# An eight-batch attention stack on one core: loads split and reordered, stacks loaded in quarters, a rewritten end, and new item orders

## The reference, cut to what matters

```python
sa = mha(x, x, swq, sbq, ..., mask=(j <= i) & (i - j < 64), bias=slopes * (j - i))
x  = layernorm(x + sa, g1, be1)
ca = mha(x, ctx, cwq, cbq, ...)                  # 512 keys, no mask
x  = layernorm(x + ca, g2, be2)
x  = layernorm(x + gelu(x @ w1 + b1) @ w2 + b2, g3, be3)
# second layer: 512 keys, a key mask
q, c = rmsnorm(x) * g_q, rmsnorm(ctx) * g_c
out  = rmsnorm(x + mha(q, c, Wq, Wk, Wv, Wo, key_mask), g_out)
```

## Time and profile before

| | |
|---|---|
| median of 3 runs | 595.97 us (595.77 to 596.03) |
| the profiled execution's own time | 598.34 us |
| span of its trace | 596.5 us |
| TensorE busy | 535.9 us, 90% of the span |
| VectorE busy | 440.7 us, 74% |
| ScalarE busy | 424.8 us, 71% |
| GpSimd busy | 340.3 us, 57% |
| mean granted TensorE clock | 0.958 of full |

### The profile page before, as it was taken

One profiled execution on the slowest core, in us unless ns is written; L12 is line 12 of the kernel. 1 busy time (PEld: TensorE's weight loads), 2 busy tenths in 40 slices (PEclk: granted clock), 3 DMA queues, 4 the chain that ended last, 5 costly groups with the idle time before them and its releaser, 6 DMA issues.

```text
span 596.5 us, 17406 instructions
## 1 busy us (share of the span) xinstructions
PE 535.9 (90%) x6868; PEld 293.6 (49%) x6868; DVE 440.7 (74%) x884; ACT 424.8 (71%) x658; POOL 340.3 (57%) x642
## 2 busy tenths in 40 slices
PE   3377989887899999999999999999999999998983
PEld 1255666663444444555554545454555444443431
DVE  6234656554989998888878788888787898989911
ACT  2135555553087887789889898989898888786782
POOL 5434578883372744646477767585858556362051
PEclk9669999996689999999999999999999999999998
DMA  6664445554515527242433435261707081643000
GB/s 175 165 162 111 112 111 150 149 159 85 134 61 123 150 31 178 92 90 96 84 116 66 129 52 144 38 157 24 174 10 178 11 184 43 137 127 47 11 12 18
DMA packets 85335, 61.08 MB, mean 102 GB/s; under 512 B 5682, under 2 KB 84834, under 8 KB 85218
## 3 DMA queue, kind: packets, MB, share of 16 engines
q1 hardware_dynamic: 85096, 59.87, 41.6%
q10 hardware_dynamic: 158, 0.10, 0.1%
HBM read 33.13 MB, written 26.22 MB: 100 GB/s over the span
## 4 chain that ended last, share of the span: by engine, by line
PE 71%; DVE 7%; DMA 6%; POOL 4%; issue 4%; ACT 2%; SPq 2%; ACTq 1%; POOLq 0%; DVEq 0%
PE pv L585 20%; PE dps L566 14%; PE aps L526 10%; PE dps L656 4%; DVE negmax L840 4%; DMA kst<-k_parts 3%; PE dps L673 3%; PE aps L638 3%; DMA qst<-mT 3%; PE aps L617 3%; DVE negmax L836 3%; PE aps L626 2%; PE dps L661 2%; PE dps L548 2%; PE aps L614 1%
## 5 line engine op out<-in xcount | busy, mean ns | idle before, releaser
L840 DVE TENSOR_REDUCE negmax<-dps 128x1 f32<-128x512 f32 x512 | 322.0, 683 | 45.0 <-PE dps L566 42.8
L708 ACT ACTIVATE probs<-aps 128x1024 f32<-128x1024 f32 x288 | 283.9, 1025 | 56.5 <-PE aps L526 31.7
L585 PE MATMUL pv<-probs,vp 128*32 128x256 f32 (+1 forms) x3072 | 160.1, 335 | 0.4 <-ACT probs L708 0.4
L566 PE MATMUL dps<-kst,qst 61*128 61x512 bf16 x512 | 123.4, 395 | 8.4 <-DMA kst<-k_parts 2.8
L526 PE MATMUL aps<-qst,kst 64*128 64x256 bf16 x1024 | 97.2, 273 | 2.3 <-ACT probs L708 1.1
L585 PEld LDWEIGHTS pv<-probs,vp 128*32 128x32 f32 x3072 | 70.9, 111 | 56.7 <-issue 27.8
L930 POOL TENSOR_SCALAR mcap<-negmax 128x16 f32<-128x16 f32 x48 | 12.1, 253 | 149.8 <-DVE negmax L840 61.7
L566 PEld LDWEIGHTS dps<-kst,qst 61*128 61x128 bf16 x512 | 32.5, 94 | 80.3 <-DVE negmax L840 62.1
L526 PEld LDWEIGHTS aps<-qst,kst 64*128 64x128 bf16 x1024 | 39.1, 94 | 48.8 <-ACT probs L708 18.7
L836 DVE TENSOR_REDUCE negmax<-dps 128x4 f32<-128x512 f32 x64 | 41.2, 686 | 23.0 <-PE dps L557 22.8
L956 POOL TENSOR_TENSOR qr<-qf,qs 128x256 f32<-128x256 f32 x24 | 16.1, 671 | 48.4 <-ACT qs L728 30.1
(11 more groups left out here) (126 smaller groups left out, 769.5 us busy)
## 6 DMA issues: line engine op xcount, KB each, us to landing
kst<-k_parts SPq DMA_DIRECT2D x32, 384.0 KB, 6.2
qst<-q_parts SPq DMA_DIRECT2D x48, 192.0 KB, 3.8
k_parts<-ks SPq DMA_DIRECT2D x16, 384.0 KB, 2.7
...
```

The lines of the kernel that those rows point to most:

```text
L566: mm = nc.tensor.matmul(dve_entry("X", u.index, n + g), q[rows_in(g, 0, ROW_M), four, tile * P:(tile + 1) * P], k[rows_in(g, 0, ROW_M), fo ...
L585: mm = nc.tensor.matmul(pv[32 * j:32 * j + 32, dst:dst + n], vp[u.parity][:, c, 4 * quad + j, :], probs[:, quad, src:src + n], start=(quad ...
L708: nc.scalar.activation(probs[:, quad, part * 1024:(part + 1) * 1024], src, ACT.Exp, scale=SCALE).then_inc(act_emptied, 1)
L840: ins = nc.vector.tensor_reduce(negmax[:, tile, at:at + 1], src, AX.X, ALU.max, negate=True)
```

## The change

Eight new order strings (only `FIRST_STEP` and `LAST_STEP` stay). The start is cut up: only the first batch's x, the identity, the first three weight matrices, two small columns and the second batch's x are issued at once by SP; `identb` and `band` go on ScalarE's queue. Stack 0's constant rows are shared between ScalarE (ones: 4 DMAs) and SP (slopes and mask: 6), stacks 1 and 2 are copied from stack 0 inside SBUF (`copy_rows`, 4 DMAs each). The other weights, the copies, the constants and x of batches 2 to 7 are issued at the head of step -1, the feed-forward weights at step 0. `load_stacks` loads `kst` with four DMAs instead of two; the first two count for `stacks_loaded`, the others for `stacks_rest`, which the ninth pair of maxima of a cross unit (the third of a self unit) waits for. `early` no longer holds for step -1. The last unit's normalisation goes to VectorE, but for the power, and its result is stored by two DMAs, one from SP and one from ScalarE.

```diff
-SECOND_STEP = "XC Q B K X X V M0 X X"
-SELF = "XC B3 Q raw K M1 S D S X P0 X V A P1 S M0 X S P2 X O"
-LAST_SELF = "XC S M1 K V B3 S X raw X Q X X X S P0 X P1 X P2 X S X X M0 X X D X X A X O X"
-CROSS_FFN = ("S X XC X S B3 S X Q X S raw sq0 M1 K X H X D X P0a A X P0b X S S F S X S P1a S X S P1b S X M0 S O "
-             "sq1 V X S sq2 P2a X T S P2b X S S X P3a")
-CROSS = ("XC S X B3 S X raw Q X K X S P0a X S M1 S D S X P0b S X S P1a X S S X P1b X sq0 V X A M0 S O S X S "
-         "P2a S X P2b X sq1 S S X T sq2 P3a X")
-NEXT_SELF = "XC B3 Q raw K M1 S D S X P0 X V A P1 S M0 X S P2 X O"
-FIRST_CROSS = ("XC S X B3 S X raw Q X K X S P0a X S M1 S D S X P0b S X S P1a X S S X P1b X sq0 V X A M0 S O S X S "
-               "P2a S X P2b X sq1 S S X T sq2 P3a X")
-LAST_CROSS = "S B3 S raw M1 S P0a S D S S P0b A S S P1a O S S P1b S S P2a S S P2b S S P3a"
+SECOND_STEP = "XC Q K X X V M0 X X B"
+SELF = "XC B3 Q raw K S M1 D X S A X P0 P1 V S M0 X S P2 X O"
+LAST_SELF = "XC Q M1 B3 K X X V X X X X S X raw S X D P0 X M0 X S X P1 X X A X X P2 X S O"
+CROSS_FFN = ("S X XC X S B3 S X Q X S M1 sq0 raw K X H X D X P0a A X P0b X S S F S X S P1a S X S P1b S X S M0 sq1 "
+             "O V S X P2a sq2 X T S X P2b X S X S P3a")
+CROSS = ("XC S X B3 S X Q X raw K S X P0a S M1 X S D S X P0b S S X P1a X S S sq0 X P1b X V X A S M0 S X O P2a "
+         "sq1 S X S P2b X S S sq2 X P3a X T")
+NEXT_SELF = "XC Q K M1 B3 S raw X S X V S D P0 M0 P1 X A X O P2 S"
+FIRST_CROSS = ("XC B3 X S sq0 S raw M1 X Q X K X S P0a X S S X D S S X P0b V X S S X P1a X A X S P1b X S S O P2a S "
+               "M0 T S X sq1 P2b X S S X P3a X sq2")
+LAST_CROSS = "S S B3 raw S M1 S S P0a S S D S P0b S S P1a S P1b S S P2a A S S P2b S P3a O"
...
+            sp.dma_start(xs[:, 0, :, :], a["x"][0].rearrange("(t p) d -> p t d", p=P)).then_inc(x_first, 16)
             sp.dma_start(ident[:, :], a["c_ident"]).then_inc(x_first, 16)
+            sp.dma_start(win[:, 0:3, :], a["w_in"][:, 0:3, :]).then_inc(win_loaded, 16)
+            for g in range(2):
+                sp.dma_start(qk_cols[rows_in(g, 0, HALF), :],
...
+            sp.dma_start(xs[:, 1, :, :], a["x"][1].rearrange("(t p) d -> p t d", p=P)).then_inc(x_second, 16)
+            sp.wait_ge(stack_zeroed[0], 2)
+            load_rows(sp)
...
-                for g in range(2):
-                    sp.dma_start(k[rows_in(g, 0, ROW_X), :, col:col + nk],
-                                 kd_rows[:, LOCAL * g:LOCAL * g + LOCAL, 0:nk]).then_inc(stacks_loaded, 16)
+                for half, loaded in enumerate((stacks_loaded, stacks_rest)):
+                    for g in range(2):
+                        first = LOCAL // 2 * half
+                        sp.dma_start(k[rows_in(g, 0, ROW_X), first:first + LOCAL // 2, col:col + nk],
+                                     kd_rows[:, LOCAL * g + first:LOCAL * g + first + LOCAL // 2, 0:nk]
+                                     ).then_inc(loaded, 16)
...
             for s in STEPS:
                 if s.i == -1:
+                    sp.dma_start(win[:, 3:9, :], a["w_in"][:, 3:9, :]).then_inc(win_rest, 16)
+                    sp.dma_start(cols[:, :], a["columns"]).then_inc(cols_loaded, 16)
+                    sp.wait_ge(ones_loaded, 64)
+                    for i in range(1, STACKS):
+                        sp.wait_ge(stack_zeroed[i], 2)
+                        copy_rows(sp, i)
+                    for dst, src in const_loads():
+                        sp.dma_start(dst, src).then_inc(consts_loaded, 16)
                     sp.dma_start(xs[:, 2:B, :, :], a["x"][2:B].rearrange("b (t p) d -> p b t d", p=P)
                                  ).then_inc(x_loaded, 16)
...
-                early = s.main is None or s.main.stage > 0
+                early = s.i == -2 or s.i >= B
...
+                if n == MAXT[u.stage] // 2:
+                    pe.wait_ge(stacks_rest, 32 * (u.index + 1))
...
+            def normalise_last(u):
+
+                chain = attn_norm
+                dve.wait_ge(chain.stats, QT * u.index + QT)
+                nc.vector.tensor_scalar(chain.ms[:, :], chain.ysum[:, :], 1.0 / D, RMS_EPS, ALU.mult, ALU.add
+                                        ).then_inc(last_root, 1)
+                dve.wait_ge(last_powered, 1)
...
+                for t in range(QT):
+                    nc.vector.scalar_tensor_tensor(chain.zg[:, t, :], chain.y[:, t, :], chain.rs[:, t:t + 1], gam[3],
+                                                   ALU.mult, ALU.mult).then_inc(last_scaled, 1)
```

141 lines of the change are left out of this document (88 added, 53 removed).

## The result

The changed kernel takes 587.61 us, median of 5 runs (583.32 to 589.04), against 595.97 us (595.77 to 597.21) before: a ratio of 0.9845 with an interval of 0.982 to 0.987. It is faster, by 1.55%, some 8.4 us, where 23.8 us were forecast; it lies 1.6 us outside the range of 563 to 586. Run again beside the experiments it took 588.25 us (584.39 to 590.49, 6 runs), ratio 0.9845 again. Its executions spread over 6 us. Those of the kernel before spread over 1.4 us beside it (5 runs), but over 5.4 us (595.52 to 600.95, 17 runs) beside the experiments, so a spread of this size isn't the changed kernel's alone.

The account below looks back on a forecast made before the run. TensorE and GpSimd were taken to bound self steps, a load wait then VectorE the border, TensorE (98.6% busy) feed-forward steps. 5.0 + 4.9 + 4.0 + 3.5 + 3.2 + 3.2 = 23.8 us off the 595.97 median: 572.2, range 563 to 586.

Parts of the forecast that it names:

- Start: Start to the end of step 0: earlier first copy and `X`, x landing at 28 to 30 us, -5.0 us.
- the load backlog eats the start: Rival at the start: x lands at 33 us or later, 5.0 falls to 0, 577 us; chance 0.12.
- Steps 1 to 6: Self steps: new orders cover TensorE's waits, 12.8 us for five steps and 13.3 for step 6, -4.9 us.
- which covers most of both: Self steps: moved `S` and `S A` cover most of TensorE's waits for GpSimd (4.7 us) and VectorE (1.5 us).
- Border: Step 7: half a `kst` ahead of the first `X` lands 3.2 us sooner, denser `X` gives -1.0; -4.0 us.
- its rival on the start and the self steps: Half clock stays into the self steps; +24 us decide, slower from three steps on; chance 0.04.
- Cross steps: Steps 8, 9, 10, 19 to 22, without feed-forward: -3.5 us in sum; hidden waits put at 1.8 us per plain step.
- feed-forward steps: Steps 11 to 18: -0.4 us each, -3.2 in sum; hidden waits put at some 2.0 us of 28.5.
- the cross orders bring nothing: Rival in the cross steps: 6.7 us of the forecast gain fall away, 579 to 585 us; chance 0.17.
- the cross orders take all: Rival in the cross steps: 12.8 and 9.0 us gained instead of 3.2 and 1.5, 559 us, half 566; chance 0.11.
- End: Step 23 gains 1.8 us, the final normalisation and stores 1.4 us; together -3.2 us.
- "A difference carries over": Whole kernel: sums made on the profiled execution, 2.4 us over the median, hold as differences for the median.

Follow-up runs that it names:

- 6: Changed kernel with x of batch 2 loaded on its own ahead of the copied stacks: 584.54 us, ratio 0.9757.
- experiment 14: Experiment 13's kernel with VectorE's preparation of the other weights put ahead of `M0` of step -1: 582.89 us, ratio 0.9743.
- 9: Experiment 6's kernel with item `B` moved from the end of step 1's order to the end of step 0's: 589.13 us, ratio 0.9853.
- 3: Changed kernel with the old orders for the self steps (`SELF`, `NEXT_SELF`, `LAST_SELF`): 587.41 us, ratio 0.983.
- 7: Changed kernel with `M1` ahead of `S` again in the self order: 587.54 us, ratio 0.9808.
- experiment 5: Kernel before with the eight new orders alone (old start, old end, `kst` in halves): 596.01 us, ratio 0.9948.
- experiment 4: Changed kernel with each `kst` loaded by two DMAs again and no second wait: 594.15 us, ratio 0.9954.
- experiment 1: Changed kernel run again with no edit: 588.25 us, ratio 0.9845.
- Experiment 12: Changed kernel with VectorE's row maxima in the cross stages reading 64 of 512 columns: 562.0 us, ratio 0.9414.
- 2: Changed kernel with the old orders for the cross steps (`FIRST_CROSS`, `CROSS`, `CROSS_FFN`, `LAST_CROSS`): 589.31 us, ratio 0.9864.
- 10: Changed kernel with the `X` matmuls of unit 8 and `K` matmuls of unit 9 issued twice: 586.32 us, ratio 0.9813.
- 15: Experiment 14's kernel with only x of batch 3 loaded in step 0, later x and feed-forward weights in step 1: 581.63 us, ratio 0.9728.
- 11: Changed kernel with the edits of experiments 9 and 10 together: 588.19 us, ratio 0.984.
- 8: Changed kernel with the `X` of the last self step spread farther: 586.79 us, ratio 0.9794.
- 13: Changed kernel with the edits of experiments 6 and 10 together: 583.27 us, ratio 0.9762.

## Why the prediction was wrong

The direction was right (0.94 for faster) and the size was not: 8.4 us in place of 23.8. Four terms were too large (start, self steps, and the two kinds of cross steps), together by 11.0 us; the border, by 2.4 us, was too small; two rivals came in part; and the sentence on how a profiled execution stands to the median was wrong by 6.7 us. By the prediction's own steps:

- *Start, -5.0 forecast, -2.0 measured.* The first half was exact: ScalarE at 5.16, first `X` at 18.47. The step that failed is "x lands at 28 to 30 us, and step 0's `XC` needs it", from which step 0 was to start at 29. It started at 31.9. x itself landed at about 31.8, and not at 28 to 30. With x there in time (6) `XC` still goes at 31.62, for the prediction saw x as the only thing ahead of it: `B` stands ahead too, waits 2.78 us for seven instructions of VectorE that begin when the last maximum is done, and would wait for the constants until 28.9 (23.82 and 5.1 us) without them, as it does until 30.1 in experiment 14. And even with `XC` at 27.8, and the 2.7 us of `B` behind it taken off, step 1 would begin at 45.0 (9): its `X` waits for the stack of batch 1 until 35.85. So the rival "the load backlog eats the start", given 0.12, took 3 us. A load by need (6) gets 3 us back: 584.54 beside 587.54 for experiment 7 in the same session.
- *Steps 1 to 6, -4.9 forecast, -0.5 measured.* The step that failed is "which covers most of both": the waits for GpSimd did fall, from 6.5 us with the old orders to 2.2, and new ones for ScalarE and VectorE took their place (3, 7). "Nothing is cheaper" stood in the text, and should have led on to the question which engine the items moved forward wait for themselves. The new orders did not shorten these steps but lengthened them, by 2.7 us with whole stacks (82.22 to 84.90, experiment 5) and by 0.6 with quarters (81.1 to 81.7, experiment 3); the -0.5 is what the quarters and the new start bring against that. Step 6 alone is 1.2 us longer with its new order (15.14 us against 13.91 in experiment 3), and holds the wait for `xc`, 0.9, and one of 0.6 for VectorE's `att`.
- *Border, -4.0 forecast.* The two terms were 3.2 for the landing and 1.0 for the order. Measured 1.9 to 2.4 for the landing (experiment 4; the mis-sized part is the time of a load that doesn't shrink with its bytes), and for the whole step 6.4 where the clock mostly held (0.94), 3.3 where it did not (0.76, step 7 of experiment 1). The forecast's -1.0 left the clock out: the earlier trace rows shows 24.08 us at 0.59, and in the changed kernel the same stretch, first `X` to step 8's `XC`, takes 20.92 us at a clock of 0.92 (133.32 to 154.24), and 24.45 at 0.71 in experiment 1. The prediction priced the slow clock in its rival on the start and the self steps alone; there steps 1 to 6 kept 1.00.
- *Cross steps, -3.5 forecast, -2.1 measured; feed-forward steps, -3.2 forecast, -1.0 measured.* The mis-sized term is the estimate of 2.0 us of hidden waits in each step. Experiment 12 measured 1.2, and the `X` rows of the profile before, which the prediction had, add up to 1.3; what else the sum took for waits is not known. A part was to come from "`O` no longer waits for VectorE"; it waits 2.2 us in the eight steps, 1.9 before. So the rival "the cross orders bring nothing", given 0.17, was nearer than the case preferred to it. The table has 3.1 us of 6.7 for these steps, and the orders account for 1.9 of them (2): in step 8 0.9 us, and in steps 19 to 22 0.4, are there with the old orders too. What the forecast gave step 10 (1.2) came, 1.07. The rival "the cross orders take all" was mis-added: 2.0 us in eight steps are 16 and not 12.8, so that by its own terms it stood at 552, half of it at 562, below the range.
- *End, -3.2 forecast, -3.0 measured.* Near in both parts: step 23 1.4 of 1.8, with ScalarE's waits down to half a microsecond, the tail 1.6 of 1.4. For the tail there is luck in it: the terms as written, 2.86 us against 1.70, give 1.2.
- *"A difference carries over"* from the profiled executions to the medians: wrong by 6.7 us. The profiled execution of before lay 2.4 us over its median; the one of after was its fastest, 4.3 under. At the border the granted clock of the 20 us behind the wait is not the same in each execution (0.92 and 0.71, experiment 1), and that makes 4.4 us. In experiments 10, 14 and 15, whose profiles show 1.00 there, the spread is 2.2, 1.8 and 1.2 us instead of 6; in 11, whose profile shows 1.00 too, it is 6.8, and no profile shows its slower executions. Experiments 6 and 8 spread over 1.5 and 2.1 us as well, with a fall at the border in their profiles, so a narrow spread alone doesn't show that the clock held. The clock at the border is shown to be one source of the difference between executions (1); whether it is the only one stays open.

Of the signs that the prediction named: first `X` near 18 (18.47) held; `XC` of step 0 near 29 failed (31.89, short of the 32 named as the limit); self steps of 12.6 to 13 failed (12.89 to 15.14), while GpSimd's wait is 2.2 over steps 1 to 6 and 1.5 from 62 to 130 us, the window of the earlier trace rows, so below 2 there; first cross `X` 19.1 behind step 6's `XC` failed (20.2 to 20.7); feed-forward steps at 28.1 failed (28.41); ScalarE without a gap in step 23 held but for waits of half a microsecond; the last store within 2 us of the last sum held (577.52 to 579.37).

What stays open: what the new start is worth in the median (4 and 5); why experiments 9 and 11 spread over 7 to 8 us; and why the clock fell in the profiled execution of 13 and not in that of 14, whose border has the same orders and the same work.
